# Rotary sine products and sums moved from GpSimd to VectorE in a two-layer recurrent kernel

## The reference, cut to what matters

```python
def rotate_half(t):
    t1, t2 = jnp.split(t, 2, axis=-1)
    return jnp.concatenate([-t2, t1], axis=-1)
...
bq = to_bhwnd(q) * dh ** (-0.5)
bk = look_around(to_bhwnd(k), LOOK_BACKWARD, LOOK_FORWARD, float(PAD_VALUE), axis=2)
...
bq = bq * jnp.cos(q_freqs) + rotate_half(bq) * jnp.sin(q_freqs)
bk = bk * jnp.cos(freqs) + rotate_half(bk) * jnp.sin(freqs)
sim = jnp.einsum('bhwid,bhwjd->bhwij', bq, bk)
```

## Time and profile before

| | |
|---|---|
| median of three runs | 5062.9 us |
| span of the profiled execution | 5060.7 us |
| busy PE (TensorE) | 4509.6 us, 89% |
| busy DVE (VectorE) | 4181.3 us, 83% |
| busy ACT (ScalarE) | 3166.3 us, 63% |
| busy POOL (GpSimd) | 2078.6 us, 41% |

### The profile page before, as it was taken

One profiled execution on the slowest core, in us unless ns is written; L12 is line 12 of the kernel. 1 busy time (PEld: TensorE's weight loads), 2 busy tenths in 40 slices (PEclk: granted clock), 3 DMA queues, 4 the chain that ended last, 5 costly groups with the idle time before them and its releaser, 6 DMA issues.

```text
span 5060.7 us, 75398 instructions
## 1 busy us (share of the span) xinstructions
PE 4509.6 (89%) x20080; PEld 2766.1 (55%) x20208; DVE 4181.3 (83%) x8946; ACT 3166.3 (63%) x6063; POOL 2078.6 (41%) x2033
## 2 busy tenths in 40 slices
PE   5679899898998989899998998989889998998989
PEld 3345555564555655555564555655555564555655
DVE  5689798888979889798888979889798888979853
ACT  2447666675766757666675766757666675666745
POOL 2234344443434444344443434444344443434423
PEclk8779999999999999999999999999999999999979
DMA  4001101111101101101111101101101111101100
GB/s 120 15 26 28 29 25 30 28 30 29 26 26 28 34 22 28 29 25 30 28 29 29 26 26 27 35 21 29 29 25 30 27 30 29 26 25 28 35 19 20
DMA packets 144530, 149.37 MB, mean 30 GB/s; under 512 B 27748, under 2 KB 107932, under 8 KB 143960
## 3 DMA queue, kind: packets, MB, share of 16 engines
q1 hardware_dynamic: 144088, 144.19, 10.9%
HBM read 22.45 MB, written 4.19 MB: 5 GB/s over the span
## 4 chain that ended last, share of the span: by engine, by line
PE 51%; DVE 27%; issue 14%; ACT 4%; POOL 1%; SPq 1%; DVEq 1%; DMA 0%; ACTq 0%; POOLq 0%
PE bT L1302 8%; DVE acc L952 8%; DVE tmp L952 6%; PE bA L1174 5%; PE bC L1359 5%; PE bU L1352 5%; PE bG L1345 4%; PE bA L1264 4%; PE bT L1314 4%; PE bT L1158 3%; DVE tmp L814 3%; PE bT L1287 2%; PE bA L1255 2%; DVE hu L1139 2%; PE bT L1327 2%
## 5 line engine op out<-in xcount | busy, mean ns | idle before, releaser
L644 POOL TENSOR_TENSOR s_h<-s_h,ge 128x512 f32<-128x512 f32 x512 | 730.2, 1426 | 1303.7 <-ACT ge L654 1052.9
L776 ACT ACTIVATE s_h<-bG 128x512 f32<-128x512 f32 x528 | 314.0, 595 | 709.9 <-DVE hu L1139 421.6
L952 DVE TENSOR_TENSOR acc<-acc,tmp 128x512 f32<-128x512 f32 x768 | 696.9, 914 | 4.2
L603 POOL TENSOR_TENSOR veA<-mvA,epsT 128x2 f32<-128x2 f32 x290 | 112.9, 389 | 1315.8 <-DVE mvA L807 1315.8
L1359 PE MATMUL bC<-hu,w_d 128*128 128x512 f32 x1056 | 582.3, 634 | 10.0 <-DVE hu L1139 9.6
L952 DVE TENSOR_TENSOR tmp<-comps 128x512 f32<-128x512 f32 x768 | 582.1, 766 | 5.8
L1302 PE MATMUL bT<-Kk,Q 64*128 64x256 f32 (+1 forms) x2048 | 545.5, 388 | 31.2 <-DVE y L1121 7.3
L753 ACT ACTIVATE probs<-bT,nmax 128x256 f32<-128x256 f32 x1024 | 413.6, 474 | 229.7 <-DVE nmax L1100 225.8
L1100 DVE TENSOR_REDUCE nmax<-bT 128x2 f32<-128x512 f32 x512 | 350.2, 685 | 194.4 <-PE bT L1302 192.3
L1314 PEld LDWEIGHTS bT<-V,probsT 128*128 128x128 f32 x3584 | 433.4, 194 | 79.6 <-issue 36.0
L1139 DVE TENSOR_TENSOR hu<-bU,s_h 128x512 f32<-128x512 f32 x528 | 360.8, 683 | 108.7 <-PE bU L1352 74.5
(11 more groups left out here) (201 smaller groups left out, 9650.8 us busy)
## 6 DMA issues: line engine op xcount, KB each, us to landing
rot<-raw SPq DMA_DIRECT2D x1024, 64.0 KB, 2.0
comps<-comps SPq DMA_DIRECT2D x384, 120.0 KB
x_ld<-in_L_attn_x SPq DMA_DIRECT2D x66, 128.0 KB, 2.2
comps<-comps SPq DMA_DIRECT2D x384, 8.0 KB
out<-O SPq DMA_DIRECT2D x16, 256.0 KB, 2.7
w_a<-in_L_attn_W_qkv SPq DMA_DIRECT2D x1, 1536.0 KB, 14.8
w_fc<-in_L_attn_fc_w SPq DMA_DIRECT2D x1, 1024.0 KB, 8.3
w_g<-in_L_ffn_w_gate SPq DMA_DIRECT2D x1, 1024.0 KB, 5.9
```

Source lines behind the costliest of these rows:

```text
L644: nc.gpsimd.tensor_tensor(s_h[:, :], s_h[:, :], ge[:, :], ALU.mult).then_inc(weighed, 1)
L776: nc.scalar.activation(s_h[:, :], bG[:, :], ACT.Silu).then_inc(silu, 1)
L952: V_.tensor_tensor(dst, i0, i1, op).then_inc(ham[h], 1)
```

## The change

VectorE's rotary step does all six operations: per tensor the product with the cosine table and at once the product with the sine table, then the two sums. GpSimd's steps q, k and rope are gone, and their letters in its order string. No other engine's string is changed, and the DMAs and semaphores keep their names and counts.

```diff
-    "pool": {"a": {"stats1", "k", "v", "q", "prep_stats", "stats2"}, "t": {"statsB", "q", "k", "rope"},
+    "pool": {"a": {"stats1", "k", "v", "q", "prep_stats", "stats2"}, "t": {"statsB"},
...
-    "pool": "aubtuababuuaututtuuattubtuauabaauubtubtuabtbuauttauabtuubtatubbtabuuaubtttuaatbatabubbtbuuttutuu"
-            "uab",
+    "pool": "aubtuababuuauuuuaubuauabaauububuabbuauauabuubaubbabuuaubuaabaabubbbuuuuuuab",
...
-                    if t[0] in "qk":
-                        i = "qk".index(t[0])
-                        pool.wait_ge(swapped[t[0]], 64 * (r.b * HP + (t[1] + 1)))
-                        nc.gpsimd.tensor_tensor(rot[:, i, :], rot[:, i, :], sinT[:, :], ALU.mult).then_inc(sin_part, 1)
-                    if t[0] == "rope":
-                        if t[1]:
-                            t_ready(pool, r, ("S", t[1] - 1, 3))
-                        for i, dst in enumerate((Q, Kk)):
-                            n = r.b * len(ROPE_ORDER) + (2 * t[1] + i + 1)
-                            pool.wait_ge(cos_part, n)
-                            pool.wait_ge(sin_part, n)
-                            nc.gpsimd.tensor_tensor(dst[:, :], raw[:, i, :], rot[:, i, :], ALU.add).then_inc(roped, 1)
...
                             V_.tensor_tensor(raw[:, i, :], raw[:, i, :], cosT[:, :], ALU.mult).then_inc(cos_part, 1)
+                            V_.tensor_tensor(rot[:, i, :], rot[:, i, :], sinT[:, :], ALU.mult).then_inc(sin_part, 1)
+                        if t[1]:
+                            t_ready(dve, r, ("S", t[1] - 1, 3))
+                        for i, dst in enumerate((Q, Kk)):
+                            n = r.b * len(ROPE_ORDER) + (2 * t[1] + i + 1)
+                            dve.wait_ge(cos_part, n)
+                            dve.wait_ge(sin_part, n)
+                            V_.tensor_tensor(dst[:, :], raw[:, i, :], rot[:, i, :], ALU.add).then_inc(roped, 1)
```

## The result

The changed kernel takes 5159.5 us, the median of four runs (5146.6 to 5174.6), against 5062.9 before. The ratio is 1.019, with a 95% interval from 1.0171 to 1.0209: slower by 97 us, where the forecast was 5067 and its range ended at 5112.

The account below looks back on a forecast made before the run. Neither TensorE (51% of the chain) nor VectorE (27%) alone was taken to bound a round. Places gave -22 us and contention +26, together +4 on a span of 5060.7; with 2.2 us from span to median, 5067 us, range 5015 to 5112.

Parts of the forecast that it names:

- Added: 0.60 us each, 307 us: On VectorE, 512 new instructions at 0.60 us from start to start: 2.4 us a pair, 307 us over the launch.
- New contention, 0.1 us each, 51 us: New VectorE instructions meet GpSimd's remaining work, above all the expert product: 3.2 us a round, half passing on, +26 us.
- Relief, 315 us: VectorE's standstills from GpSimd's rotary work go: 2.5 us a pair, 315 us in the launch, bounded by 180 and 548.
- rival 2: The relief wins: VectorE gains 159 us, at 27% of the chain 43 us, giving 5020 us; chance 0.31.
- First, third, fourth and eighth pair, -3.5 us a round: Path effect by place: first pair -0.2, third and fourth -2.0 for both, eighth -1.3 us a round.
- Fifth and sixth pair, +2.1 us a round: Where TensorE bounds: +4.8 added, -2.1 relief, less 0.62 idle; 2.1 us late at a normalisation TensorE already awaits.
- Rival 3: Added cost passes on where TensorE reaches its wait before the relief: +2.5 us a round, 40 us, 5103; chance 0.32.
- Rival 4: Expert products wait behind the burst and stand where rotary ones stood: +40 us, 5103 or more; chance 0.03.
- What would show it: Signs named beforehand: instruction means, VectorE and GpSimd busy times, TensorE's normalisation waits; a time outside 5015 to 5112 refutes the view.

Follow-up runs that it names:

- without the burst: Kernel before the change with GpSimd's sine products and sums cut to one column of 512, nothing added to VectorE: 4772.1 us.
- the 387 us of cost: Changed kernel, 5159.5 us, less the kernel before with GpSimd's rotary operations cut to one column, 4772.1 us.
- both tries: Bursts of pairs five and six later in the changed kernel, 5186.8 us; second pair's burst behind unit 8's hidden part in the 5018 us kernel, 5065.8 us.
- two kernels whose waits were 351 and 357 us in all: Changed kernel with pairs five and six back on GpSimd, 5018.3 us; the same with the second pair's burst later in VectorE's order, 5065.8 us.

## Why the prediction was wrong, point by point

- *Added: 0.60 us each, 307 us.* Right: five of the six in a burst start 0.60 us after one another.
- *New contention, 0.1 us each, 51 us.* Right in sum: the new instructions' means lie over 682 ns by 24 us in the sine products and 32 in the `Kk` sums, 56 together. VectorE's busy time rose by 23 us where I had 43. But the contention is not spread: 30 standstills of 1.07 us fall on the `Kk` sum, all at the two places with little room, and nearly all of the 24 us on the third and fourth pair. Letting half of it pass on everywhere put 1.6 us a round in the sum and nothing at the two places.
- *Relief, 315 us.* Right, 310 on the engine. On the time it was worth 291 us without the burst. The forecast went by places and passed nearly all of it on; rival 2 priced VectorE's gain at the chain's 27%, and against 291 of 310 that share is far too low.
- *First, third, fourth and eighth pair, -3.5 us a round.* Not wrong in kind: with the fifth and sixth on GpSimd the rest gains 45 us, 2.8 a round, where 3.5 less the contention's 1.6 had it at 1.9. The parts don't bear the places out, though: the first four alone gain 9 us and the last two 6, so the near agreement of the sum is partly luck.
- *Fifth and sixth pair, +2.1 us a round.* **This is the step that failed.** I took 2.1 us of relief off the 4.8, let the two pairs' lateness pass on once, at a normalisation for which TensorE waited already, and charged the path nothing for a collision just there. The first result behind each burst is another one, the scaled `acc` and `xr`, for which TensorE didn't wait before, and I never looked at how much time these had to spare. The relief was in the wrong place for them: the normalisation of 2.09 us starts at 2325.48, behind the `xr` of 2321.49. The runs show 2.4 + 1.07 - 0.96 = 2.5 us at the fifth pair and 2.4 + 1.07 - 0.80 = 2.7 at the sixth, 78 us in the launch (82.4 - 4.6), and behind these waits the lower clock, 52 us more of TensorE's busy time (my estimate from 26 drops at 1.5 us is 39; some last twice as long as the one shown). Together that is the 130 us between the traces of 5018 and 5160, and 141 us between their medians, 8.8 a round, in place of 16 x 2.1 = 34. The account closes: the two pairs cost 107 us more than forecast, the six others brought 45 in place of 30, and the forecast was missed by 92.
- *Rival 3, the burst passes on and the relief doesn't, 5103.* It had the burst right, but the wrong half beside it: the relief did pass on. With 1.05 us a pair at these two places it was too low by the factor 2.5, and it had no clock in it.
- *Rival 4, products stand where rotary operations stood.* Its sign was there at 0.03: the expert product went from 730.2 to 802.8 us, and `hu` waits for it 45.0 us (29.4 before):

```profile
DVE hu L1134 <- POOL s_h L631: 45.0, 36, 3.1
```

Without six products beside the bursts the changed kernel takes 149 us less.

- *What would show it.* `acc` 796 (about 800), normalisation 389 (under 550), VectorE 4204 (4180 to 4260), GpSimd 1409 (up to 1350, missed by the starved products), sine products 777, sums 680 and 931 (0.70 to 0.80; over 0.9 means contention, and it did). TensorE's wait for the normalisation did not grow near the sixth pair; the wait there is for `xr`. The time left the range, and as stated the waits had moved to where I did not look.

What the experiments leave open: how the 387 us of cost are split between the six other pairs, and what moves the granted clock between kernels with about equal waits. That the clock drops because of the wait is an inference from the counts; no kernel changed the clock with the waits held. The products were only cut, never moved, so what a product costs by its own place and what by meeting a burst is separated only where the trace shows the standstill, at the fifth and sixth pair.

## What to carry to other kernels

An exchange that comes out even in an engine's busy time can still cost, because the relief and the new work fall on different places: find, for each burst that you lengthen, the next result behind it that a fuller engine waits for, and how much time it has to spare. Half of a change, or the change at six of eight places, is worth a run: here six of eight places took 5018 us and half of the change 5048, both below the 5063 of the kernel before, where the whole took 5160. Moving such a burst in a hand-laid order can exchange one late result for another, as both tries here did. And compare TensorE's granted clock beside its waits: two kernels whose waits were 351 and 357 us in all were 47 us apart.

## What the runs showed of the hardware

- GpSimd can lose the shared resource over a whole row of VectorE instructions: its product, begun at 2214.94, took 4.56 us in place of 1.26, while the six instructions of the burst and a quaternion product behind them, all with two on-chip inputs, followed each other every 0.60 us until 2218.38; none of them was longer for it. That happened once in each of the 15 middle rounds. Where it came to the last of such a row, at 2328.72, it was VectorE that stood still, and its own time was 1.32.
- The Trainium skill, "SBUF — State Buffer", section "Who interferes with whom", says that issue order, not the kind of operation, decides who blocks. The fifth pair's rows agree with that. The second pair's don't suit a simple reading of it: there GpSimd started before four of the six, and still ended last.
- At the two places above, TensorE's waits of 2.52 and 2.67 us were followed by the lower clock level in 26 of 30 cases, waits of 1.44 and 1.60 us in 3 of 30. Such drops made the same 20208 instructions busy for 52 us longer.
- The four runs of the changed kernel spread over 28 us, those of the kernel before beside them over 2; why is not shown.
